# Setup as a stage of the pipeline, and the queries' root inside the exponentials of the local attention

## The chip, the cores and the metric

The kernel runs on one core of a Trainium2 chip. Its five engines are TensorE (PE, with its weight loads shown apart as PEld), VectorE (DVE), ScalarE (ACT), GpSimd (POOL) and SyncE (SP, which here only issues DMAs). Each has its own queue of instructions, works it off in order, and waits for others on semaphores. The metric is the device time of one execution in microseconds; lower is better. A kernel that differs by less than 0.3% from another isn't told from it.

## The reference

The input x has 16 sequences of 256 tokens of width 128, in fp32. Two layers, each a gated cross attention and a gated feed-forward part, with residuals:

```
x1 = x  + tanh(g_xattn[0]) * cross0(LN(x), ctx)         # 16 heads of 8, a mask on the keys
x2 = x1 + tanh(g_ffn[0])   * ffn0(LN(x1))
x3 = x2 + tanh(g_xattn[1]) * cross1(LN(x2), ctx)        # with biases
x4 = x3 + tanh(g_ffn[1])   * experts(LN(x3))            # 8 experts, the best 2, squared relu
```

ffn0 is itself a transformer of two layers. The part that matters here is its local attention, 8 heads of 64, over windows of 64 tokens, each looking at itself and the window before:

```
q, k, v = split(shift(h) @ wqkv)
q = q / |q| * q_scale ;  k = k / |k| * k_scale     # norm over each head's 64 values
q, k = rotate(q), rotate(k)                        # q also times 8
sim  = q . k, far and later positions masked
out  = softmax(sim) . v ;  h = h + out @ wo
```

## The kernel before

The 4096 tokens are 32 tiles of 128 (T = 32). Six stages work over all tiles: cross 0, local 0, mlp 0, local 1, mlp 1, cross 1, and the experts as a seventh. One loop over steps drives all engines (L1406 to L1454). Each stage has a start step (0, 34, 68, 104, 138, 173, 208), and in step s of a stage each of its operations works on tile n = s - offset; the offset is written in the code (`n = s - 5`). So each engine's queue is an order written out by hand: within a step the later stages come first, and within a stage the blocks stand in the order of the code. Stages overlap only at their ends, while one runs out and the next fills.

Ahead of the loop stands the setup (class Setup): SP and ACT issue all loads, PE makes keys and values of the context for both layers, DVE masks them. Its weights wait for one semaphore of 8 transfers, and every engine waits in `settle` for all that the setup does before it enters the loop.

The local attention on one tile (class Local), by engine, at the offsets of the kernel before:

- PE: transposes h (L839, s-1); projects queries and keys into `a_ps_qk`, three matmuls of 512 columns each (L790 to L792, s-2); transposes the rotated queries and keys (L875, s-4); projects the values (s-4); lays the mask and the scores into `a_ps_s` (L823, L806, s-5); transposes the exponentials (L847, s-6); multiplies with the values (L863, s-7); the output projection (L896, s-8).
- ACT: copies, two squares of the projections (L939, L951), and the exponentials (L932): eight instructions of 128x128, one for each head, each with a bias from `a_stat` and a sum into it.
- DVE: the rotation, four multiplies of 512 columns (L1037, L1039) and an add for the queries (L1013); the sums of squares (L988); the greatest score (L995); the inverse of the sums (L1024); copies.
- POOL: the add of the rotated keys (L1059), the roots (L1061, L1063: a power over 16 columns), the multiply of rotated queries and keys by their roots (L1067, 1024 columns), and the multiply of the exponentials by the inverse sums (L1073, 1024 columns).

The lines that set the exponentials and the multiply by the roots:

```python
act.activation(self.e[n % 2][:, P * i:P * i + P], ps_s[:, P * i:P * i + P], ACT.Exp,
               bias=stat[:, i:i + 1], accum_out=stat[:, 8 + i:9 + i]).then_inc(self.s_e, 1)
...
r = self.rot[n % 2][:, :].rearrange("p (h d) -> p h d", d=LD)
p.tensor_tensor(r, r, t[:, 48:64].unsqueeze(2).broadcast_to([P, 16, LD]), ALU.mult).then_inc(self.s_n, 1)
```

`a_ps_s` and `a_ps_t` each exist once in each layer, so the scores of a tile wait until the exponentials of the tile before have been read (`after(pe, self.s_e, 8 * k)`), and the two kinds of transposes take turns.

## Time and profile before

| | |
|---|---|
| median of 3 runs | 1317.49 us (1314.54 to 1318.94) |
| the profiled execution | 1315.28 us, its span 1313.5 us |
| mean granted TensorE clock | 0.962 of full |
| PE busy | 1142.4 us, 87% |
| PEld | 967.6 us, 74% |
| DVE | 1020.3 us, 78% |
| ACT | 913.0 us, 70% |
| POOL | 886.1 us, 67% |

The shares are means over stages with different limits: the setup is over after about 43 us, cross 0 runs to about 190 us, local 0 to about 500, mlp 0 to about 590, local 1 to about 870, and mlp 1, cross 1 and the experts fill the rest. An instruction's duration is longer than the distance to the next one on its engine, since neighbours overlap; where engines are compared, starts are what counts. Idle time of an engine that nobody waits for costs nothing.

### The profile page before, as it was taken

Reading aid. Unit: us, or ns where it says so; the run is one execution under the profiler, and the core shown is the slowest. Engines: PE = TensorE matmul, PEld = TensorE weight load, DVE = VectorE, ACT = ScalarE, POOL = GpSimd, SP = SyncE. Lnnn points to the kernel's source line nnn. Section 1 sums busy time; section 2 is a strip of 40 time slices with the busy share of each in tenths; the row PEclk is TensorE's granted clock in tenths of the full one; section 3 lists DMA queues with packets and bytes.
Section 4 is the critical chain, followed back from the end, with each engine's and each line's share of the span. In section 5 each row is a group of like instructions: output and inputs, shape, how many; then the busy total and the mean of one; then the engine's idle time right before and its main releaser. Section 6 shows DMA issues by size and latency. Waiting matters only on the chain.

```text
span 1313.5 us, 34022 instructions
## 1 busy us (share of the span) xinstructions
PE 1142.4 (87%) x11792; PEld 967.6 (74%) x11792; DVE 1020.3 (78%) x2334; ACT 913.0 (70%) x2541; POOL 886.1 (67%) x1108
## 2 busy tenths in 40 slices
PE   5388886799999988886999999979979999999997
PEld 3277764577777768885777777769867777999997
DVE  2699986788888866677888888848878887588887
ACT  1399983787777875455887777755578888666664
POOL 0688865999999983229999999943376764333442
PEclk8699997999999998997999999999989999899999
DMA  6100000000000000210011000001100000000000
GB/s 173 53 9 2 1 2 9 9 10 10 10 9 9 12 2 19 62 26 10 10 26 58 10 9 15 2 7 30 24 1 1 2 1 1 6 13 13 14 12 15
DMA packets 59417, 23.34 MB, mean 18 GB/s; under 512 B 49093, under 2 KB 57202, under 8 KB 59250
## 3 DMA queue, kind: packets, MB, share of 16 engines
q1 hardware_dynamic: 55296, 19.22, 6.0%
q10 hardware_dynamic: 3954, 1.96, 0.6%
q8 instruction: 98, 1.61, 0.5%
q14 instruction: 69, 0.57, 0.1%
HBM read 10.68 MB, written 2.10 MB: 10 GB/s over the span
## 4 chain that ended last, share of the span: by engine, by line
PE 36%; ACT 20%; DVE 19%; issue 12%; POOL 10%; ACTq 1%; DMA 1%; SPq 1%; DVEq 0%; POOLq 0%
ACT a_e L932 11%; PE m_ps_h L1275 7%; PE m_ps_y L1287 7%; DVE a_rot L1037 6%; DVE a_rot L1039 3%; PE x_ps_t L495 3%; PE a_ps_t L847 3%; ACT a_sq L939 2%; ACT x_khm L552 2%; DVE a_stat L995 2%; POOL a_stat L1063 2%; PE f_ps_y L1132 2%; POOL a_e L1073 2%; PE f_ps_g L1143 2%; PE x_ps_s L452 2%
## 5 line engine op out<-in xcount | busy, mean ns | idle before, releaser
L1063 POOL TENSOR_TENSOR a_stat<-a_stat,small 128x16 f32<-128x16 f32 x64 | 187.7, 2934 | 5.3
L932 ACT ACTIVATE a_e<-a_ps_s,a_stat 128x128 f32<-128x128 f32 x512 | 180.2, 379 | 3.2 <-DVE a_stat L995 2.4
L1073 POOL TENSOR_TENSOR a_e<-a_e,a_stat 128x1024 f32<-128x1024 f32 x64 | 121.5, 1898 | 20.0 <-DVE a_stat L1024 20.0
L1067 POOL TENSOR_TENSOR a_rot<-a_rot,a_stat 128x1024 f32<-128x1024 f32 x64 | 121.9, 1904 | 5.2 <-DVE a_rot L1013 0.3
L932 ACT ACTIVATION_READ_ACCUMULATOR a_e<-a_ps_s,a_stat 128x1 f32 x512 | 111.5, 218 | 0.0
L1037 DVE TENSOR_TENSOR a_rot<-a_ps_qk,a_rtab 128x512 f32<-128x512 f32 x128 | 87.8, 686 | 28.3 <-ACT a_sq L939 27.8
L925 ACT ACTIVATE a_eT<-a_ps_t 128x1024 f32<-128x1024 f32 x64 | 65.5, 1024 | 59.7 <-PE a_ps_t L847 57.1
L1059 POOL TENSOR_TENSOR a_rot<-a_rot 128x512 f32<-128x512 f32 x64 | 82.1, 1283 | 36.2 <-DVE a_rot L1039 34.3
L1173 ACT ACTIVATE f_gl<-f_ps_g,vec 128x128 f32<-128x128 f32 (+1 forms) x192 | 55.9, 361 | 62.7 <-PE f_ps_g L1143 62.7
L1275 PE MATMUL m_ps_h<-m_hT,w 128*128 128x128 f32 x768 | 95.1, 281 | 0.0
L1287 PE MATMUL m_ps_y<-w,m_up 128*128 128x128 f32 x768 | 91.1, 275 | 1.5 <-DVE m_yw L1322 1.5
L638 DVE TENSOR_REDUCE x_stat<-x_ps_s 128x16 f32<-128x1024 f32 x64 | 78.4, 1224 | 17.8 <-PE x_ps_s L453 17.6
L1275 PEld LDWEIGHTS m_ps_h<-m_hT,w 128*128 128x128 f32 x768 | 89.9, 195 | 0.0
L1287 PEld LDWEIGHTS m_ps_y<-w,m_up 128*128 128x128 f32 x768 | 88.3, 192 | 1.6 <-issue 1.6
L1039 DVE TENSOR_TENSOR a_rot<-a_ps_qk,a_rtab 128x512 f32<-128x512 f32 x128 | 87.1, 681 | 0.0
L1308 ACT ACTIVATE m_up<-m_ps_h 128x512 f32<-128x512 f32 x96 | 57.1, 598 | 42.3 <-PE m_ps_h L1275 42.3
L495 PE MATMUL x_ps_t<-c,x_e 128*128 128x128 f32 x512 | 73.2, 288 | 13.2 <-ACT x_e L558 13.2
L995 DVE TENSOR_REDUCE a_stat<-a_ps_s 128x8 f32<-128x1024 f32 x64 | 77.8, 1216 | 8.2 <-PE a_ps_s L806 8.2
L875 PE MATMUL a_ps_t<-c,a_rot 128*128 128x128 f32 x512 | 70.3, 282 | 15.6 <-POOL a_rot L1067 4.9
L847 PE MATMUL a_ps_t<-c,a_e 128*128 128x128 f32 x512 | 69.7, 280 | 14.6 <-POOL a_e L1073 14.5
L261 POOL TENSOR_SCALAR f_st<-f_st 128x1 f32<-128x1 f32 x64 | 14.3, 223 | 96.3 <-DVE f_st L256 95.0
L261 POOL TENSOR_SCALAR m_st<-m_st 128x1 f32<-128x1 f32 x32 | 7.3, 227 | 105.4 <-DVE m_st L256 105.4
(168 smaller groups left out, 3726.3 us busy)
## 6 DMA issues: line engine op xcount, KB each, us to landing
a_h<-y SPq DMA_DIRECT2D x64, 32.0 KB
f_h<-y SPq DMA_DIRECT2D x64, 32.0 KB
out_dram<-x SPq DMA_DIRECT2D x32, 64.0 KB, 1.5
a_h<-y SPq DMA_DIRECT2D x64, 31.8 KB
f_h<-y SPq DMA_DIRECT2D x64, 31.8 KB
wqkv<-in_L_ffn_wqkv_dram SPq DMA_DIRECT2D x2, 768.0 KB, 4.8
w<-in_L_ffn_w_dram SPq DMA_DIRECT2D x2, 768.0 KB, 5.2
c_ctx2T<-in_ctxT_dram SPq DMA_DIRECT2D x2, 512.0 KB, 3.2
```

The lines of the kernel that those rows point to most:

```text
L495: m = pe.transpose(ps_t[:, P * i:P * i + P], self.e[n % 2][:, P * i:P * i + P], g.ident)
L847: m = pe.transpose(ps_t[:, P * i:P * i + P], self.e[n % 2][:, P * i:P * i + P], g.ident)
L932: act.activation(self.e[n % 2][:, P * i:P * i + P], ps_s[:, P * i:P * i + P], ACT.Exp, bias=stat[:, i:i + 1], accum_out=stat[:, 8 + i:9 + ...
L995: v.tensor_reduce(self.stat[n % 2][:, 0:8], ps_s[:, :].rearrange("p (r k) -> p r k", k=P), AX_X, ALU.max, negate=True).then_inc(self.s_mx, 1)
L1037: v.tensor_tensor(out1, qk, cos_.unsqueeze(1).broadcast_to([P, LH, LD]), ALU.mult).then_inc(self.s_r, 1)
L1039: v.tensor_tensor(out2.rearrange("p h (o d) -> p h o d", o=2), swapped, sin_.rearrange("p (o d) -> p o d", o=2).unsqueeze(1).broadcast_to( ...
L1059: p.tensor_tensor(r, r, self.rot2[:, INNER:], ALU.add).then_inc(self.s_n, 1)
L1063: p.tensor_tensor(t[:, 48:64], t[:, 32:48], g.neg_half.broadcast_to([P, 16]), ALU.pow).then_inc(self.s_n, 1)
L1067: p.tensor_tensor(r, r, t[:, 48:64].unsqueeze(2).broadcast_to([P, 16, LD]), ALU.mult).then_inc(self.s_n, 1)
L1073: p.tensor_tensor(e3, e3, self.stat[n % 2][:, 16:24].unsqueeze(2).broadcast_to([P, 8, P]), ALU.mult)\
L1275: m = pe.matmul(self.ps_h[b][:, P * i:P * i + P], g.w1[:, P * c:P * c + P], self.hT[n % 2][:, :], start=True, stop=True)
L1287: m = pe.matmul(self.ps_y[:, D * e:D * e + D], self.up[n % 2][:, P * c:P * c + P], g.w2[:, D * c:D * c + D], start=(i == 0), stop=(i == w ...
```

## The change

It has three parts.

First, Setup becomes a stage of the loop at start 0, whose pieces stand behind those of cross 0 in steps -3 to 4. The one semaphore for weights and the `settle` ahead of the loop are gone; each consumer waits for its own load (`setup.s_id`, `setup.s_x[i]`, `setup.s_wq[l]`, ...). The local stage alone settles, on its first steps. The context is loaded once instead of twice, the masks as single rows instead of 128 copies, x in three parts; the values come in products of 128 columns, four to a bank, and layer 1's mask and key bias go into its key product as a masked context and a row of the bias.

Second, in the local attention POOL multiplies only the keys by their roots (512 columns). The queries go on unscaled; DVE multiplies the negated greatest scores by the queries' roots (8 columns), and the exponentials take that as bias and the root as scale. The mask becomes -1e24, and `a_stat` has four buffers instead of two.

Third, the blocks of the local stage stand in another sequence and at other offsets: the loads two steps ahead, all other work one step earlier, the projection of queries and keys in two blocks with their own waits. The starts of the stages become 0, 35, 67, 103, 135, 170, 205.

In the diff: the setup's products on PE, then of the local stage PE's blocks whose waits are new, ACT's exponentials, DVE's new multiply, POOL's multiply by the roots, and at the end the starts of the stages.

```diff
+    def product_k(self, pe, l, i):
+        g, src = self.g, (self.ctxT, self.ctxm)[l]
+        for j in range(2):
+            at = slice(512 * j, 512 * j + 512)
+            if l:
+                pe.matmul(self.ps_k[l][i][:, at], self.bk[:, P * i:P * i + P], self.mrow[:, at], start=True, stop=False)
+            m = pe.matmul(self.ps_k[l][i][:, at], g.wk[l][:, P * i:P * i + P], src[:, at], start=not l, stop=True)
+        m.then_inc(self.s_k, 1)
+
+    def product_v(self, pe, l, q, ps):
+
+        if l:
+            pe.matmul(ps, self.g.ones_row[:, :], self.bv[:, :].unsqueeze(1).broadcast_to([1, 4, D]), start=True, stop=False)
+        for i in range(4):
+            b = 4 * q + i
+            for lo, at, n in ((0, SC * b - SC, P),) if b else ((0, SC * (B - 1), SC), (SC, 0, SC)):
+                m = pe.matmul(ps[lo:lo + n, D * i:D * i + D], self.ctxT[:, at:at + n], self.wv[l][:, :], start=not l, stop=not l or i == 3)
+        return m
+
+    def tensor(self, pe, l, s):
+        g = self.g
+        if s == -3:
+            pe.wait_ge(self.s_key, 48)
+            for i in range(2):
+                self.product_k(pe, 0, i)
+            pe.wait_ge(self.s_val, 16)
+            for q in range(2):
+                self.product_v(pe, 0, q, self.ps_v0[q]).then_inc(self.s_vp, 1)
+        if s == 0:
+            pe.wait_ge(self.s_clear, 1)
+            pe.wait_ge(self.s_mr, 1)
+            pe.wait_ge(self.s_kl, 1)
+            for j in range(2):
+                at = slice(512 * j, 512 * j + 512)
+                m = pe.matmul(self.ps_a[:, at], g.ones_row[:, :], self.mrow[:, at], start=True, stop=True)
+            m.then_inc(self.s_bc, 1)
+            pe.wait_ge(self.s_kl, 2)
+            for q in (2, 3):
+                self.product_v(pe, 0, q, self.ps_v0[q]).then_inc(self.s_vp, 1)
+        if s in (1, 2):
+            if s == 1:
+                pe.wait_ge(self.s_val1, 32)
+            for i in range(2):
+                q = 2 * (s - 1) + i
+                if s == 1:
+                    pe.wait_ge(self.s_ve, 3 + i)
+                else:
+                    pe.wait_ge(self.s_v1, 1 + i)
+                self.product_v(pe, 1, q, self.ps_v1[q]).then_inc(self.s_vq, 1)
+        if s == 2:
+            pe.wait_ge(self.s_key1, 64)
+            pe.wait_ge(self.s_cm, 1)
+            pe.wait_ge(self.s_ve, 2)
+            self.product_k(pe, 1, 0)
+        if s == 3:
+            pe.wait_ge(self.s_kl, 3)
+            self.product_k(pe, 1, 1)
...
+        end = T * l + T
         if s == 0:
+            if not l:
+                settle(pe, self.setup.totals())
             pe.wait_ge(self.s_wh, l + 1)
             pe.wait_ge(self.s_wr, l + 1)
-        n = s - 5
+        n = s - 4
+        if 0 <= n < T:
+            k = T * l + n
+            after(pe, self.s_vc, k)
+            after(pe, self.s_oc, k - 2)
+            if n == 0:
+                self.take(pe, l, "b")
+            self.project_h(pe, ps_b[:, :], n, 1024).then_inc(self.s_v, 1)
+        n = s - 7
+        if 0 <= n < T:
+            k = T * l + n
+            pe.wait_ge(self.s_oc, k + 1)
+            after(pe, self.s_yc, k)
+            pe.wait_ge(self.s_hc, min(k + 7, end))
+            pe.wait_ge(self.s_hr, min(k + 7, end))
+            for pair in range(LP):
+                m = pe.matmul(ps_a[:, 0:D], self.oT[n % 2][:, P * pair:P * pair + P], g.lwo[:, D * pair:D * pair + D],
+                              start=(pair == 0), stop=(pair == LP - 1))
+            m.then_inc(self.s_y, 1)
...
         if 0 <= n < T:
             k = T * l + n
+            pe.wait_ge(self.s_hc, k + 1)
+            pe.wait_ge(self.s_hr, k + 1)
+            after(pe, self.s_sq, 2 * (k - 1) + 1)
+            after(pe, self.s_r, 4 * (k - 1) + 2)
+            if n == 0:
+                self.take(pe, l, "qk")
+            self.project_h(pe, ps_qk[:, 0:INNER], n, 0).then_inc(self.s_qk, 1)
+        n = s - 3
+        if 0 <= n < T:
+            k = T * l + n
+            pe.wait_ge(self.s_n, 4 * k + 4)
+            pe.wait_ge(self.s_nq, k + 1)
+            after(pe, self.s_ec, k - 2)
+            after(pe, self.s_qc, k)
+            after(pe, self.s_kc, k)
+            if n == 0:
+                self.take(pe, l, "t")
+            for i in range(2 * LP):
+                m = pe.transpose(ps_t[:, P * i:P * i + P], self.rot[n % 2][:, P * i:P * i + P], g.ident)
+            m.then_inc(self.s_t, 1)
...
+        n = s - 5
+        if 0 <= n < T:
+            k = T * l + n
+            pe.wait_ge(self.s_en, k + 1)
+            pe.wait_ge(self.s_qc, min(k + 3, end))
+            pe.wait_ge(self.s_kc, min(k + 3, end))
...
-            self.project_h(pe, ps_b[:, :], n, 1024).then_inc(self.s_v, 1)
+            self.project_h(pe, ps_qk[:, INNER:], n, INNER).then_inc(self.s_qk, 1)
...
+        n = s - 4
+        if 0 <= n < T:
+            k, stat = T * l + n, self.stat[n % UNROLL]
+            act.wait_ge(self.s_mx, 3 * k + 2)
+            after(act, self.s_et, k - 1)
+            for i in range(2 * LP):
+                e, pair = divmod(i, LP)
+                root = 48 + 2 * pair + e
+                act.activation(self.e[n % 2][:, P * i:P * i + P], ps_s[:, P * i:P * i + P], ACT.Exp, bias=stat[:, 24 + i:25 + i],
+                               scale=stat[:, root:root + 1], accum_out=stat[:, 8 + i:9 + i]).then_inc(self.s_e, 1)
...
-            act.wait_ge(self.s_mx, 2 * k + 1)
-            after(act, self.s_et, k - 1)
-            for i in range(2 * LP):
-                act.activation(self.e[n % 2][:, P * i:P * i + P], ps_s[:, P * i:P * i + P], ACT.Exp,
-                               bias=stat[:, i:i + 1], accum_out=stat[:, 8 + i:9 + i]).then_inc(self.s_e, 1)
...
+            v.wait_ge(self.s_mx, 3 * k + 1)
+            v.wait_ge(self.s_n, 4 * k + 2)
+            v.tensor_tensor(stat[:, 24:32].rearrange("p (e r) -> p e r", e=2), stat[:, 0:8].rearrange("p (e r) -> p e r", e=2),
+                            stat[:, 48:56].rearrange("p (r e) -> p e r", e=2), ALU.mult).then_inc(self.s_mx, 1)
...
-            r = self.rot[n % 2][:, :].rearrange("p (h d) -> p h d", d=LD)
-            p.tensor_tensor(r, r, t[:, 48:64].unsqueeze(2).broadcast_to([P, 16, LD]), ALU.mult).then_inc(self.s_n, 1)
...
+            r = self.rot[n % 2][:, INNER:].rearrange("p (h d) -> p h d", d=LD)
+            p.tensor_tensor(r, r, t[:, 56:64].unsqueeze(2).broadcast_to([P, LH, LD]), ALU.mult).then_inc(self.s_n, 1)
...
-        for stage, l, later in ((cross, 0, 0), (local, 0, T + 2), (mlp, 0, T + 2), (local, 1, T + 4), (mlp, 1, T + 2),
+        for stage, l, later in ((setup, 0, 0), (cross, 0, 0), (local, 0, T + 3), (mlp, 0, T), (local, 1, T + 4), (mlp, 1, T),
                                 (cross, 1, T + 3), (experts, 0, T + 3)):
             start += later
```

ACT in the middle of local 0, one step of the kernel before:

```order
L932 ACTIVATE a_e,a_stat<-a_ps_s,a_stat 128x128 x8
L939 ACTIVATE a_sq<-a_ps_qk 128x512
L945 ACTIVATE a_kTr<-a_ps_t 128x4x128
L951 ACTIVATE a_sq<-a_ps_qk 128x512
L961 ACTIVATE a_vt<-a_ps_b 128x512
L919 ACTIVATE a_hT<-a_ps_a 128x128
L925 ACTIVATE a_eT<-a_ps_t 128x1024
```

and one step of the changed kernel, where L1041 is the copy of the keys, L1048 that of h, and L1057 the exponentials:

```order
L1041 ACTIVATE a_kTr<-a_ps_t 128x4x128
L1048 ACTIVATE a_hT<-a_ps_a 128x128
L1057 ACTIVATE a_e,a_stat<-a_ps_s,a_stat 128x128 x8
L1064 ACTIVATE a_sq<-a_ps_qk 128x512
L1070 ACTIVATE a_eT<-a_ps_t 128x1024
L1028 ACTIVATE a_vx<-a_ps_b 64x512
L1029 ACTIVATE a_vt<-a_ps_b 128x512
L1035 ACTIVATE a_sq<-a_ps_qk 128x512
```

The exponentials have moved from behind the copy of the transposed exponentials to ahead of it, and the copies of keys and of h stand ahead of them.

PE at the same place, the kernel before, from the transposes of the rotated tile to the next tile's:

```order
L875 MATMUL a_ps_t<-c,a_rot 128x128 x8
L790 MATMUL a_ps_qk<-a_wqh,a_hT 128x512
L791 MATMUL a_ps_qk<-a_wqr,a_hT 128x512
L792 MATMUL a_ps_qk<-a_wqh,a_hTr 128x512
L790 MATMUL a_ps_qk<-a_wqh,a_hT 128x512
L791 MATMUL a_ps_qk<-a_wqr,a_hT 128x512
L792 MATMUL a_ps_qk<-a_wqh,a_hTr 128x512
L896 MATMUL a_ps_a<-lwo,a_oT 128x128 x4
```

and in the changed kernel, where L941 and L902 are the mask and the scores, L886 to L888 the projection, L969 the transposes of the rotated tile and L994 the product with the values:

```order
L941 MATMUL a_ps_s<-c 128x512 x2
L902 MATMUL a_ps_s<-a_kTr,a_qT 64x128 x16
L886 MATMUL a_ps_qk<-a_wqh,a_hT 128x512
L887 MATMUL a_ps_qk<-a_wqr,a_hT 128x512
L888 MATMUL a_ps_qk<-a_wqh,a_hTr 128x512
L969 MATMUL a_ps_t<-c,a_rot 128x128 x8
L994 MATMUL a_ps_b<-a_eT,a_vt 64x64 x16
L1005 MATMUL a_ps_t<-c,a_e 128x128 x8
L886 MATMUL a_ps_qk<-a_wqh,a_hT 128x512
L887 MATMUL a_ps_qk<-a_wqr,a_hT 128x512
L888 MATMUL a_ps_qk<-a_wqh,a_hTr 128x512
```

Between scores and transposes of the rotated tile now stands the queries' half of the projection alone; the keys' half has moved behind the transposes of the exponentials. No matmul of the local stage is added or lost.

## Rows read from the trace of the kernel before

**Rows 1.** The page's first part: busy time of each engine

```profile
PE 1142.4 (87%) x11792; PEld 967.6 (74%) x11792; DVE 1020.3 (78%) x2334; ACT 913.0 (70%) x2541; POOL 886.1 (67%) x1108
```

**Rows 2.** Timeline of the first 60 us: start us, us, engine, line, instruction

```profile
13.18 3.60 PE L346 MATMUL c_ps_k<-c_ctx2T,wk 128*128 128x512 f32 x8
...
24.83 6.36 PE L346 MATMUL c_ps_k<-c_ctx2T,wk 128*128 128x512 f32 x8 [5.89 <-DVE kT L361]
...
53.75 0.77 PE L452 MATMUL x_ps_s<-x_khl,x_qhh 128*128 128x512 f32 x1 [0.76 <-DVE x_qlm L652]
```

**Rows 3.** DMA issues: KB each, median us to landing

```profile
wk<-in_L_xattn_WkT_dram ACTq DMA_DIRECT2D x4, 64.0 KB, 6.0
```

**Rows 4.** Timeline of POOL: first and last root multiply of each layer

```profile
213.36 1.91 POOL L1067 TENSOR_TENSOR a_rot<-a_rot,a_stat 128x1024 f32<-128x1024 f32 x1
...
481.64 1.90 POOL L1067 TENSOR_TENSOR a_rot<-a_rot,a_stat 128x1024 f32<-128x1024 f32 x1
...
597.35 1.90 POOL L1067 TENSOR_TENSOR a_rot<-a_rot,a_stat 128x1024 f32<-128x1024 f32 x1
...
858.49 1.90 POOL L1067 TENSOR_TENSOR a_rot<-a_rot,a_stat 128x1024 f32<-128x1024 f32 x1
```

**Rows 5.** Timeline of POOL over one step of local 1

```profile
612.56 1.90 POOL L1073 TENSOR_TENSOR a_e<-a_e,a_stat 128x1024 f32<-128x1024 f32 x1
614.41 1.27 POOL L1059 TENSOR_TENSOR a_rot<-a_rot 128x512 f32<-128x512 f32 x1
...
615.99 2.93 POOL L1063 TENSOR_TENSOR a_stat<-a_stat,small 128x16 f32<-128x16 f32 x1
618.99 1.91 POOL L1067 TENSOR_TENSOR a_rot<-a_rot,a_stat 128x1024 f32<-128x1024 f32 x1
```

**Rows 6.** Timeline of PE in local 0, with idle time ahead in brackets

```profile
302.82 0.47 PE L790 MATMUL a_ps_b<-a_wqh,a_hT 128*128 128x512 f32 x1
...
303.61 0.60 PE L823 MATMUL a_ps_s<-c 128*128 128x512 bf16 x2
...
305.82 0.30 PE L839 MATMUL a_ps_a<-c,a_h 128*128 128x128 f32 x1 [0.58 <-DVE y L1045]
...
308.22 1.06 PE L875 MATMUL a_ps_t<-c,a_rot 128*128 128x128 f32 x8
...
312.11 0.60 PE L823 MATMUL a_ps_s<-c 128*128 128x512 bf16 x2
```

**Rows 7.** Timeline of DVE in the same step, its two waits

```profile
311.04 0.20 DVE L1024 RECIPROCAL a_stat<-a_stat 128x8 f32<-128x8 f32 x1 [1.01 <-ACT a_e L932]
311.63 0.69 DVE L1037 TENSOR_TENSOR a_rot<-a_ps_qk,a_rtab 128x512 f32<-128x512 f32 x1 [0.38 <-ACT a_sq L939]
```

**Rows 8.** Timeline of ACT: a tile's first exponential, and what follows the eighth

```profile
299.47 0.37 ACT L932 ACTIVATE a_e<-a_ps_s,a_stat 128x128 f32<-128x128 f32 x1
...
302.23 0.64 ACT L939 ACTIVATE a_sq<-a_ps_qk 128x512 f32<-128x512 f32 x1
302.70 0.65 ACT L945 ACTIVATE a_kTr<-a_ps_t 128x512 f32<-128x512 f32 x1
```

**Rows 9.** Groups of ACT by shape: count, busy us, mean ns, idle before

```profile
L932 ACT ACTIVATE a_e<-a_ps_s,a_stat 128x128 f32<-128x128 f32 x512 | 180.2, 379 | 3.2 <-DVE a_stat L995 2.4
L932 ACT ACTIVATION_READ_ACCUMULATOR a_e<-a_ps_s,a_stat 128x1 f32 x512 | 111.5, 218 | 0.0
...
L1165 ACT ACTIVATE f_hT<-f_ps_x,vec 128x128 f32<-128x128 f32 x64 | 29.3, 458 | 14.0 <-PE f_ps_x L1122 13.8 <-issue 0.2
...
L566 ACT ACTIVATE x_qhh<-x_ps_q,small 128x128 fp32r<-128x128 f32 x64 | 19.8, 360 | 8.3 <-PE x_ps_q L464 8.2
...
L919 ACT ACTIVATE a_hT<-a_ps_a 128x128 fp32r<-128x128 f32 x64 | 17.7, 277 | 73.4 <-PE a_ps_a L839 73.3
```

**Rows 10.** Timeline of ACT while mlp 0 runs alone

```profile
530.45 0.88 ACT L1173 ACTIVATE f_gl<-f_ps_g,vec 128x128 f32<-128x128 f32 x3 [0.88 <-PE f_ps_g L1143]
...
532.55 0.87 ACT L1173 ACTIVATE f_gl<-f_ps_g,vec 128x128 f32<-128x128 f32 x3 [0.88 <-PE f_ps_g L1143]
```

548 lines of the change are left out of this document (273 added, 275 removed).

## Prediction

> **What bounds the kernel now.** I read the page's first part first [rows 1]: PE 87%, DVE 78%, ACT 70%, POOL 67%. These are means over seven stages, so they don't say what bounds the local attention, where most of the change lies. The timeline does. POOL's multiply by the roots starts at 213.36 us for the first tile of local 0 and at 481.64 for the last; in local 1 at 597.35 and 858.49 [rows 4]. These are 31 steps each: 268.3 / 31 = 8.65 us a step and 261.1 / 31 = 8.42. In such a step POOL hardly rests [rows 5]: from the multiply of the exponentials at 612.56 it is 1.85 us to the add, 1.58 to the power (a small maximum lies between), 3.00 to the multiply by the roots, and that multiply takes 1.86 to its follower, 8.29 in all. So POOL bounds the local attention, and with 62 steps of some 8.5 us it is 40% of the time.
>
> The other three are close behind. PE comes from one tile's masks at 303.61 to the next one's at 312.11 in 8.50 us, of which one wait on DVE is 0.58 [rows 6]; as every block also begins with a gap of some tenths, I take 7.8 us as the least PE needs. DVE waits 1.01 and 0.38 us in a step [rows 7], so it needs 8.50 - 1.39 = 7.1. ACT does the eight exponentials in 302.23 - 299.47 = 2.76 us [rows 8], and its idle time in a step is about 1.5 us, so it needs 6.9 to 7.0 (an estimate from its timeline; the row of the copy of h alone has 73.4 us of idle over 64 steps, 1.15 each [rows 9]).
>
> The start is a chain of its own [rows 2]: key products from 13.18 us on, the second layer's only at 24.83, at half the clock (6.36 us for what took 3.60), and then masks; the first scores of cross 0 come at 53.75 us.
>
> **The local step after the change.** POOL: the multiply by the roots falls from 1024 to 512 columns. Half of 1.90 is 0.95, the least; the add of the same 512 columns with two full inputs takes 1.27 [rows 5], the most. The row nearest in kind is the multiply with a repeated operand, so I take 0.97 and POOL's sum is 8.29 - 0.90 = 7.4 us (7.35 to 7.7).
>
> DVE: one more multiply of 8 columns. The nearest row is the reciprocal of 8 columns, 0.20 us [rows 7]; it must also wait for the maximum just before it to be written. I take 0.25 (0.1 to 0.4): 7.35 us.
>
> ACT: the exponentials get a second operand from SBUF. The trace has no exponential with both, but it has 128x128 instructions from PSUM with none, one and two such operands: 277, 360 and 458 ns [rows 9]. So the scale costs 98 ns each, 8 x 0.098 = 0.78 us a step, 3.54 instead of 2.76. The bounds: 0, if the read of the accumulator (218 ns, half hidden now) covers it; 2.0 us, if the pair of 379 + 218 ns no longer overlaps. I take the row's 0.78, and ACT's sum is 7.7 us. So most of what POOL is spared in time (0.90 a step) is paid again on ACT; it is hidden only as far as ACT idled.
>
> The Trainium skill, "ScalarE: Activation LUTs", in the part on what an ACT_TABLE_LOAD costs, has a rule that speaks against this edit: each per-partition pointer operand of an ACTIVATE adds about 93 ns. By it the sum for ACT would be 8 x 0.093 = 0.74 us a step. It agrees with the three rows; that the price also holds in time to the next instruction, and for an exponential with a sum, no run here shows.
>
> PE: the same matmuls in the local stage, one more block to start: 7.8 to 7.9. Its wait for DVE's addition to y (0.58) goes, since the output projection now stands well ahead of the transpose of h that needs its bank.
>
> So POOL 7.4, DVE 7.35, ACT 7.7, PE 7.8: level, and what decides is the chain between them. Follow a tile from its masks at 0. Masks and scores end at 305.24 - 303.61 = 1.63 (the wait before 305.82 began then). The queries' half of the projection adds 0.79 (the three value matmuls from 302.82 to 303.61 are the same kind), the eight transposes 1.06 (0.8 to the next block), all [rows 6]: they end at about 3.4. Then ACT copies the keys (0.47 to the next, as at 302.23 to 302.70 [rows 8]) and h (0.2), and starts the exponentials at 4.1; the greatest scores (1.2 us behind the scores) and the new multiply are ready by 3.2, so they are off this chain. 3.54 later, at 7.65, the eighth is done, and with 0.1 for the semaphore the next masks may start: 7.75. PE comes to the same point at 7.8. DVE's own round, entered by its wait for the same transposes, gives 7.75 too. In the kernel before, the exponentials also stood behind the copy of the transposed ones, which waits for POOL's multiply; that dependence is gone, which is why the step can follow POOL down at all.
>
> With all four level each small delay of one is felt by all; I add 0.15 and forecast 7.95 us a step (bounds 7.5, where only the sums of POOL and DVE count, and 8.4, where the exponentials cost 0.5 more). Local 0 runs its first five steps beside the end of cross 0, whose own root operations on POOL stay, so it keeps some 3 us: 268.3 - 31 x 7.95 - 3 = 19; local 1: 261.1 - 31 x 7.95 = 15. Sum 34 us.
>
> **The setup.** The first scores need: the key weights (issued by ACT first now; a landing takes 6.0 us [rows 3], so PE starts near 7.5 instead of behind eight transfers), then PE's work. A 512-column matmul in fp32 costs 3.60 / 4 = 0.90 us at the full clock and 6.36 / 4 = 1.59 at the lower [rows 2]. Ahead of the first scores stand 4 key products for layer 0, 4 for layer 1 with their bias rows, 2 to spread the mask row, 4 rows of value bias: 14 x 0.90 = 12.6, and 34 value products of 128 columns at a quarter, 7.6. That is 20 us, against 14.4 before; the price of the new form is 6 us of PE. The waits between (mask rows landed, the low parts of the keys, DVE's masked values before their banks are free) add 4 to 5. So the first scores come at 32 at the full clock and at 44 if half of it runs at the lower. I take 36, and lose 1.5 again as the last four key products (3.6 us) now lie among the first steps of cross 0, whose PE is not full. Gain 53.75 - 36 - 1.5 = 16 us; bounds 8 and 22. The final `settle` of the local stage, 30 steps later, waits for nothing.
>
> What SP queues now ahead of the attention weights (some 30 issues instead of 9) is needed at step 4 of cross 0 or later, and the attention weights at step 32: hidden, 0; should x's second part be late, cross 0 waits 1 to 3 us once.
>
> **The ends of the stages.** The loop has three steps less. Each makes one step in which an mlp ran alone one that is shared with the local attention. Alone such a step takes 532.55 - 530.45 = 2.10 us [rows 10]: 6.3 us, less about 2 for the work that now lies in a fuller step. I take 4 (bounds 10 and -4; the conversion of the attention weights, now two and three steps earlier, falls into cross 0's full steps instead of an emptier one).
>
> **Sum.** From the profiled execution: 1315.28 - 34 - 16 - 4 = 1261 us, and its median's scale is 0.2% higher; I stay with 1261.
>
> **The rivals.**
>
> 1. The step falls to the sums of POOL and DVE, 7.5 us: the semaphore gaps that I counted on PE overlap, and the scale is half hidden behind the accumulator's read. For it: four banks of statistics and earlier loads give slack. Against it: PE's 7.8. Local saving 529.4 - 62 x 7.5 - 3 = 61: 1315 - 61 - 16 - 4 = 1234.
> 2. ACT keeps the old pace. The exponentials cost 1.2 us more instead of 0.78, since the new operand can't be read while the accumulator is; the chain masks, projection, transposes, copies, exponentials becomes 8.3. Local saving 529.4 - 62 x 8.35 - 3 = 9: 1286.
> 3. Slower: the same chain at its worst. If ACTIVATE and accumulator read no longer overlap, eight pairs take 8 x (379 + 98 + 218) = 5.6 us, the step 4.1 + 5.6 + 0.1 = 9.8, and the local stages lose 62 x (9.8 - 8.54) = 78: about 1373. It turns to slower than before where the step exceeds 8.54 + 20 / 62 = 8.86, that is where a pair costs over 0.58 us instead of 0.345 now. Against it: the rows with one and two operands differ by 98 ns and not by more.
> 4. The setup doesn't shorten: PE idles long enough between its pieces to run at the lower clock throughout, as from 24.83 us now, and DVE's chain of waits does the rest. First scores at 48, gain 4: 1273.
>
> **Chances.** The forecast 0.60 (own range 1246 to 1276), rival 1 0.14, rival 2 0.14, rival 4 0.06, rival 3 0.04, and 0.02 for no change by two errors that cancel. What a measurement can tell from no change is 0.3%, 4 us. Faster 0.94, same 0.02, slower 0.04. The range leaves out rival 3 and the outer part of 1 and 2: 1230 to 1290.
>
> **What would show it.** Right: starts of the keys' root multiply 7.8 to 8.1 us apart in both local stages, that multiply near 0.97 us, the exponentials near 475 ns and eight of them in 3.5 us, PE's wait for y gone and its idle time in local 0 under 5%, POOL busy for less than 7.6 us of a step there; first scores at 32 to 44 us. Wrong: a step at 8.4 with ACT busy throughout (rival 2), a step at 7.5 (rival 1), or stretches of cross 0 slower than before by more than 3 us, which I counted at nothing.

## The result, and the profile after

| | kernel before | changed kernel |
|---|---|---|
| median of the runs shown | 1316.39 us (1314.54 to 1318.94, 4 runs) | 1271.01 us (1258.75 to 1272.81, 4 runs) |
| profiled execution | 1315.28 us, span 1313.5 | 1272.81 us, span 1270.9 |
| mean granted clock of TensorE | 0.962 | 0.960 |

The ratio is 0.9641, with a 95% interval of 0.9608 to 0.9673: 45 us faster. I had forecast 1261 us, so the time lies 10 us above it, inside both ranges. One of the four runs was at 1258.75 us, with a mean clock of 0.974 where the others had 0.960 to 0.967; that difference inside one kernel gave the first hint of the cause below.

The page's first part after, to set beside [rows 1]. PE has 24.5 us more of busy time, for 56 more instructions; that is more than their work.

```profile
PE 1166.9 (92%) x11848; PEld 983.7 (77%) x11848; DVE 1026.1 (81%) x2368; ACT 955.8 (75%) x2545; POOL 859.6 (68%) x1110
```

The timeline of POOL, first and last multiplication of the keys by their root in each layer, as in [rows 4]:

```profile
214.56 1.38 POOL L1200 TENSOR_TENSOR a_rot<-a_rot,a_stat 128x512 f32<-128x512 f32 x1
...
464.57 1.04 POOL L1200 TENSOR_TENSOR a_rot<-a_rot,a_stat 128x512 f32<-128x512 f32 x1
...
572.94 1.04 POOL L1200 TENSOR_TENSOR a_rot<-a_rot,a_stat 128x512 f32<-128x512 f32 x1
...
818.39 1.04 POOL L1200 TENSOR_TENSOR a_rot<-a_rot,a_stat 128x512 f32<-128x512 f32 x1
```

These four starts and the span cut both kernels into the same five pieces, and the differences add up to the whole:

| piece | before | after | difference | forecast |
|---|---|---|---|---|
| start to the first such multiplication (setup, cross 0) | 213.4 | 214.6 | +1.2 | -16 |
| 31 steps of local 0 | 268.3 | 250.0 | -18.3 | -19 |
| from local 0 to local 1 (mlp 0) | 115.7 | 108.4 | -7.3 | -4, with the last piece |
| 31 steps of local 1 | 261.1 | 245.4 | -15.7 | -15 |
| from there to the end of the span | 455.0 | 452.5 | -2.5 | |

So the local attention gave what was forecast, the ends of the stages gave more, and the setup gave nothing. Over 31 steps the local attention goes from 8.65 to 8.06 us a step in local 0, and from 8.42 to 7.92 in local 1; in the middle of both stages it goes from 8.57 to 7.86. The first steps of the stages make the difference.

**The step of the local attention.** POOL over one step, as in [rows 5]:

```profile
299.49 1.44 POOL L1200 TENSOR_TENSOR a_rot<-a_rot,a_stat 128x512 f32<-128x512 f32 x1
300.90 1.89 POOL L1182 TENSOR_TENSOR a_e<-a_e,a_stat 128x1024 f32<-128x1024 f32 x1
302.76 0.24 POOL L1189 TENSOR_SCALAR a_stat<-a_stat 128x16 f32<-128x16 f32 x1
303.09 2.92 POOL L1192 TENSOR_TENSOR a_stat<-a_stat,small 128x16 f32<-128x16 f32 x1
305.98 1.29 POOL L1194 TENSOR_TENSOR a_rot<-a_rot 128x512 f32<-128x512 f32 x1
307.36 1.44 POOL L1200 TENSOR_TENSOR a_rot<-a_rot,a_stat 128x512 f32<-128x512 f32 x1
```

307.36 - 299.49 = 7.87 us, and POOL doesn't wait. PE in the same step, as in [rows 6]:

```profile
299.86 0.59 PE L941 MATMUL a_ps_s<-c 128*128 128x512 bf16 x2
...
302.22 1.03 PE L969 MATMUL a_ps_t<-c,a_rot 128*128 128x128 f32 x8
303.09 0.27 PE L980 MATMUL a_ps_a<-c,a_h 128*128 128x128 f32 x1
...
307.72 0.59 PE L941 MATMUL a_ps_s<-c 128*128 128x512 bf16 x2
```

From masks to masks 7.86 us, and no row has a wait in brackets: the 0.58 us for DVE's addition to y [rows 6] is gone. Two engines without a pause in one step don't tell which of them sets it; that takes an experiment. DVE's one wait of note in that step, to set beside [rows 7], and the addition of the rotated queries, which now begins 0.16 us before POOL's multiplication:

```profile
303.29 0.69 DVE L1133 COPY a_qT<-a_ps_t 128x512 f32<-128x512 f32 x1 [0.31 <-PE a_ps_t L969]
...
307.20 0.69 DVE L1164 TENSOR_TENSOR a_rot<-a_rot 128x512 f32<-128x512 f32 x1
```

ACT's first exponential and what follows the eighth, as in [rows 8]; and its groups by shape, as in [rows 9]:

```profile
303.94 0.46 ACT L1057 ACTIVATE a_e<-a_ps_s,a_stat 128x128 f32<-128x128 f32 x1
...
307.42 0.64 ACT L1064 ACTIVATE a_sq<-a_ps_qk 128x512 f32<-128x512 f32 x1
```

```profile
L1057 ACT ACTIVATE a_e<-a_ps_s,a_stat 128x128 f32<-128x128 f32 x512 | 226.7, 477 | 4.5 <-DVE a_stat L1126 4.4
L1057 ACT ACTIVATION_READ_ACCUMULATOR a_e<-a_ps_s,a_stat 128x1 f32 x512 | 115.8, 226 | 0.0
```

Eight exponentials take 3.48 us (2.76 before; forecast 3.54). One takes 477 ns, 98 more than before. The other two groups of rows hardly differ: the key weights land after 4.5 us (6.0 in [rows 3]), and a step of the mlp alone takes 2.11 us (2.10 in [rows 10]).

**The start.** PE in the first 60 us, to set beside [rows 2]. `1*128 1x512` is a product of one row: a bias, or the mask's row, spread over a tile. The trace records each fp32 product of the setup as two instructions, so `x2` is one product of 512 columns.

```profile
25.95 2.07 PE L349 MATMUL c_ps_b<-c_bv,ones_row 1*128 1x512 f32 x2 [0.75 <-ACT vall L410]
27.95 2.08 PE L353 MATMUL c_ps_b<-c_wv,c_ctxT 128*128 128x128 f32 x8
...
39.98 2.08 PE L343 MATMUL c_ps_c<-c_ctxm,wk 128*128 128x512 f32 x2
41.06 1.42 PE L531 MATMUL x_ps_s<-x_khl,x_qhh 128*128 128x512 f32 x1
...
47.70 2.07 PE L342 MATMUL c_ps_c<-c_mrow,c_bk 1*128 1x512 f32 x2 [3.52 <-DVE kT L421]
```

The first scores stand at 41.06 us, 12.7 earlier than before. But the gain is gone one tile later. DVE's maxima of the first three tiles of cross 0, before and after:

```profile
55.83 1.23 DVE L638 TENSOR_REDUCE x_stat<-x_ps_s 128x16 f32<-128x1024 f32 x1 [1.77 <-PE x_ps_s L453]
60.00 1.22 DVE L638 TENSOR_REDUCE x_stat<-x_ps_s 128x16 f32<-128x1024 f32 x1 [0.94 <-PE x_ps_s L453]
64.03 1.22 DVE L638 TENSOR_REDUCE x_stat<-x_ps_s 128x16 f32<-128x1024 f32 x1 [0.94 <-PE x_ps_s L453]
```

```profile
43.66 1.23 DVE L729 TENSOR_REDUCE x_stat<-x_ps_s 128x16 f32<-128x1024 f32 x1 [17.38 <-PE x_ps_s L532]
57.35 1.22 DVE L729 TENSOR_REDUCE x_stat<-x_ps_s 128x16 f32<-128x1024 f32 x1 [8.04 <-PE x_ps_s L532]
62.97 1.22 DVE L729 TENSOR_REDUCE x_stat<-x_ps_s 128x16 f32<-128x1024 f32 x1 [0.93 <-PE x_ps_s L532]
```

12.2 us ahead at the first tile, 1.1 at the third. Between them stand the last key products, from 47.70 us on. They first wait 3.52 us, then run at half the clock. The wait is a chain through one place in PSUM: both halves of layer 1's keys go through `c_ps_c`, so PE may write the second half only when ACT has copied the first and DVE has subtracted that copy, and ACT comes to this behind its copies for the first tile and of the values:

```profile
45.34 1.05 ACT L397 ACTIVATE kT<-c_ps_c 128x1024 fp32r<-128x1024 f32 x1
46.41 1.23 DVE L421 TENSOR_TENSOR kT<-c_ps_c,kT 64x1024 fp32r<-64x1024 f32 x1 [1.21 <-ACT kT L397]
```

The windows of 26 to 42 and 42 to 58 us after (length, then busy us of PE, PEld, DVE, ACT, POOL, then TensorE's granted clock, DMA share, GB/s):

```profile
26.00:42.00 16.00, 16.00 (x29) 7.00 (x30) 0.24 (x2) 1.98 (x4) 5.41 (x8) 0.50 0.24 60
42.00:58.00 16.00, 12.48 (x30) 6.03 (x29) 5.03 (x7) 4.19 (x8) 2.27 (x7) 0.64 0.00 0
```

PE works 16.00 of 16.00 us, and is granted 0.50, the level of 1.2 GHz. The Trainium skill, "TensorE: Matmul & The Clock Gate", section "Why this matters for your kernels", advises to keep TensorE busy without a pause for the full rate. This trace differs, and the measurement decides: the stretch has no pause. What sets it apart from stretches at 1.00 may be what PE works on; the experiments below test that.

### The profile page after: what moved, and what is told of

Read it like the earlier page. It is cut to its first block, busy times and chain, and to the rows that moved or that the text cites. A ratio compares the mean times of both kernels' runs of the same rounds, so it can differ in the third digit from the quotient of the medians.

```text
span 1270.9 us, 34469 instructions
## 1 busy us (share of the span) xinstructions
PE 1166.9 (92%) x11848; PEld 983.7 (77%) x11848; DVE 1026.1 (81%) x2368; ACT 955.8 (75%) x2545; POOL 859.6 (68%) x1110
## 4 chain that ended last, share of the span: by engine, by line
PE 71%; ACT 8%; DVE 7%; issue 7%; POOL 4%; SPq 1%; DMA 1%; ACTq 0%; DVEq 0%; POOLq 0%
PE m_ps_h L1401 7%; PE m_ps_y L1413 7%; PE a_ps_s L902 5%; PE a_ps_b L994 5%; PE a_ps_t L1005 5%; PE a_ps_t L969 4%; PE a_ps_a L929 4%; PE a_ps_qk L886 3%; PE x_ps_t L575 3%; PE a_ps_s L941 2%; ACT x_khm L636 2%; PE a_ps_qk L888 2%; PE a_ps_qk L887 2%; PE x_ps_s L531 2%; PE f_ps_g L1269 2%
## 5 line engine op out<-in xcount | busy, mean ns | idle before, releaser
L1057 ACT ACTIVATE a_e<-a_ps_s,a_stat 128x128 f32<-128x128 f32 x512 | 226.7, 477 | 4.5 <-DVE a_stat L1126 4.4
L1057 ACT ACTIVATION_READ_ACCUMULATOR a_e<-a_ps_s,a_stat 128x1 f32 x512 | 115.8, 226 | 0.0
L1200 POOL TENSOR_TENSOR a_rot<-a_rot,a_stat 128x512 f32<-128x512 f32 x64 | 90.1, 1407 | 5.0
L1194 POOL TENSOR_TENSOR a_rot<-a_rot 128x512 f32<-128x512 f32 x64 | 82.9, 1296 | 7.2 <-DVE a_rot L1080 7.1
L1115 DVE TENSOR_REDUCE a_stat<-a_sq 128x16 f32<-128x1024 f32 x64 | 77.8, 1215 | 1.2 <-ACT a_sq L1064 1.1
L575 PEld LDWEIGHTS x_ps_t<-c,x_e 128*128 128x128 f32 x512 | 57.1, 145 | 27.5 <-ACT x_e L642 19.8
L902 PEld LDWEIGHTS a_ps_s<-a_kTr,a_qT 64*64 64x64 f32 x2048 | 55.8, 134 | 27.9 <-issue 27.9
```

The source lines that it names most:

```text
L575: m = pe.transpose(ps_t[:, P * i:P * i + P], self.e[n % 2][:, P * i:P * i + P], g.ident)
L902: return pe.matmul(dst, self.qT[u][rows, P * pair + WIN * x:P * pair + WIN * x + WIN], ky, start=False, stop=(pair == LP - 1))
L1194: p.tensor_tensor(r, r, self.rot2[:, INNER:], ALU.add).then_inc(self.s_n, 1)
L1200: p.tensor_tensor(r, r, t[:, 56:64].unsqueeze(2).broadcast_to([P, LH, LD]), ALU.mult).then_inc(self.s_n, 1)
```

## The experiments

Each kernel is the changed kernel with one edit, unless it says otherwise. In the local attention I read the step as the mean distance of POOL's multiplications of the exponentials over some 16 steps in the middle of each layer, since the total also carries what the clock does at the start.

### The two parts apart

`local_alone` is the kernel before with the class of the local attention, the mask's constant and the starts of the stages from the changed one:

```
...
-((cross, 0, 0), (local, 0, T + 2), (mlp, 0, T + 2), (local, 1, T + 4), (mlp, 1, T + 2),
+((cross, 0, 0), (local, 0, T + 3), (mlp, 0, T), (local, 1, T + 4), (mlp, 1, T),
...
```

> The kernel before with the changed local attention alone (its order on each engine, the root as scale, the mask's constant, the starts of the stages), and the setup of before. If the gains of the two parts add up as the stretches of the two traces say (18.3 and 15.6 us in the two local stages, 7.5 between local and MLP of layer 0, 2.5 in the rest), this takes 1271 to 1275 us, since the setup gave 1.5 us there and took 2.7 us back at the start of the local stage. Had the setup's part given what I forecast (16 us), and the local part less, it would be 1283 to 1287 us.

Measured: 1269.23 us (1267.82 to 1270.01), ratio 0.9639 [0.9622, 0.9655]. That is the whole gain of the change, from the local part and the starts alone. Its five pieces are 213.7, 250.0, 107.9, 245.8 and 450.2 us. So the new setup as it stands is worth nothing, and its cost isn't hidden somewhere later either. No run tells the two halves of the local part apart, the root as scale of the exponentials and the new order of the blocks: what each is worth of the 34 us isn't shown.

### What holds the setup back

`rows128` gives the one-row products 128 rows, 127 of them zeros:

```
-self.ones_row = sb("ones_row", P, F32, 1)
+self.ones_row = sb("ones_row", P, F32)
...
-self.bv, self.bk = self.sb("bv", D, F32, 1), self.sb("bk", 2 * D, F32, 1)
+self.bv, self.bk = self.sb("bv", D, F32), self.sb("bk", 2 * D, F32)
...
+for t in (self.bv, self.bk, self.mrow):
+    v.memset(t[:, :], 0.0).then_inc(self.s_zr, 1)
...
-pe.matmul(ps, self.g.ones_row[:, :], self.bv[:, :].unsqueeze(1).broadcast_to([1, 4, D]), ...)
+pe.matmul(ps, self.g.ones_row[:, :], self.bv[:, :].unsqueeze(1).broadcast_to([P, 4, D]), ...)
...
```

> The changed kernel with one edit in the setup: the products that spread a row (the mask's row, and layer 1's biases of keys and values) take 128 rows, the row itself and 127 rows of zeros, in place of one row. Columns and output are the same; three VectorE memsets are added. Theory A (the granted clock): in the changed kernel PE works without a pause from about 26 to 57 us but is granted 0.50 in most of it, and the stretches at 0.50 are those with one-row products; with 128 rows the clock is 1.0 from about 30 us on, the second tile's statistics come some 8 to 14 us earlier, and the kernel takes 1257 to 1263 us. Rival B (the work): the setup's stage is as long as its products and the waits between engines make it, rows or not; then nothing moves, 1269 to 1273 us, and the clock stays at 0.50 in the same stretches.

Measured: 1258.42 us (1257.97 to 1258.87), ratio 0.9557 [0.9542, 0.9573], so 11 to 13 us less than the changed kernel (by the ratios, and by the medians), with more work in it. Its windows:

```profile
26.00:42.00 16.00, 12.48 (x39) 6.61 (x38) 4.38 (x6) 5.27 (x10) 7.42 (x16) 0.89 0.36 100
42.00:58.00 16.00, 12.62 (x110) 10.22 (x111) 12.66 (x24) 12.10 (x22) 9.37 (x17) 0.89 0.01 3
```

and the products at its start:

```profile
25.88 1.02 PE L351 MATMUL c_ps_b<-c_bv,ones_row 128*128 128x512 f32 x2
26.74 1.05 PE L355 MATMUL c_ps_b<-c_wv,c_ctxT 128*128 128x128 f32 x8
...
36.23 2.06 PE L344 MATMUL c_ps_c<-c_mrow,c_bk 128*128 128x512 f32 x2 [3.52 <-DVE kT L423]
38.09 1.82 PE L345 MATMUL c_ps_c<-c_ctxm,wk 128*128 128x512 f32 x2
39.75 1.02 PE L344 MATMUL c_ps_c<-c_mrow,c_bk 128*128 128x512 f32 x2
```

The same product takes 1.02 us where it took 2.07. From 22 us on the clock falls only behind PE's two long waits, the 3.52 us ahead of 36.23 and one of 3.01 us ahead of 47.00, and each time it comes back among the matmuls that follow. The first scores are at 30.67 us and the first multiplication by the root at 200.8: 10.4 and 13.7 us ahead of the changed kernel. Against the kernel before, the first piece is 12.6 us shorter, where I had forecast 16.

The clock isn't all that the start lacks. DVE's maxima of the first and the third tile of cross 0 in `rows128`:

```profile
32.20 1.22 DVE L734 TENSOR_REDUCE x_stat<-x_ps_s 128x16 f32<-128x1024 f32 x1 [7.84 <-PE x_ps_s L537]
...
49.08 1.23 DVE L734 TENSOR_REDUCE x_stat<-x_ps_s 128x16 f32<-128x1024 f32 x1 [1.81 <-PE x_ps_s L537]
```

These are 16.9 us apart, against 8.2 in the kernel before and 19.3 in the changed one. So of the 11.1 us of lead that the changed kernel loses between them, 8.7 are lost with 128 rows too: the wait for `c_ps_c`, which is 3.52 us here as well, the key products themselves, and the next wait. The clock costs 2.4 us there, and most of its price, 10.4 us, lies ahead of the first scores.

`rows1ctl` is the control: the tiles, memsets and waits of `rows128`, with the products back on one row.

```
...
-self.bk[:, P * i:P * i + P], self.mrow[:, at]
+self.bk[0:1, P * i:P * i + P], self.mrow[0:1, at]
...
```

> Control for rows128: the same tiles of 128 rows, the same three memsets, the same wait ahead of the loads of the biases, but the products take the first row alone. Theory A (a one-row product doesn't hold the granted clock up): the clock is back at 0.50 from 26 to 57 us and the time is that of the changed kernel, 1268 to 1273 us. Rival F (rows128 gained by the memsets' or loads' moved times, or by where the products fell): 1257 to 1261 us as rows128.

Measured: 1270.30 us (1269.26 to 1271.83), ratio 0.9665 [0.9636, 0.9695], and its windows are back near where they were, at 0.60 and 0.54:

```profile
26.00:42.00 16.00, 15.73 (x37) 7.54 (x37) 1.43 (x3) 2.33 (x6) 5.95 (x10) 0.60 0.38 108
42.00:58.00 16.00, 12.06 (x25) 5.89 (x25) 5.70 (x8) 5.72 (x11) 3.71 (x8) 0.54 0.00 0
```

Its first scores are at 37.97 us and its first and third maxima 21.0 us apart (40.70 and 61.71), so against this control the clock costs 7.3 us ahead of the first scores and 4.1 between those maxima. So it is the rows and nothing that came with them. Theory A holds; rivals B and F fall.

`nobias` leaves the eight bias products out:

```
-    pe.matmul(self.ps_k[l][i][:, at], self.bk[:, P * i:P * i + P], self.mrow[:, at], start=True, stop=False)
...
-    pe.matmul(ps, self.g.ones_row[:, :], self.bv[:, :].unsqueeze(1)..., start=True, stop=False)
```

> The changed kernel without layer 1's bias rows in the products of keys and values (8 one-row products of 512 columns left out of the computation). Theory A (the granted clock, as for rows128): the one-row product that spreads the mask stays, the others go, so the clock comes back by about 35 us and 8 products of 1.04 us at full clock go as well; the kernel takes 1253 to 1261 us, less than with 128 rows. Rival B (the work): only the 8 products go, at 2.07 us each from the trace 16.6 us, and the clock stays at 0.50 in the rest; 1254 to 1262 us. The clock of the stretch from 30 to 55 us tells them apart, not the time.

Measured: 1250.24 us (1248.57 to 1254.02), ratio 0.9499 [0.9477, 0.9521]. The two windows show 0.76 and 0.81 instead of 0.50 and 0.64, so the clock is up for part of the stretch, as theory A has it. It falls behind PE's waits of 3.52 us (until 31.98) and 3.02 us (until 42.08), with no one-row product near: waits and rows both bring it down. Its first piece is 195.7 us, 5.1 us less than in `rows128`, for eight products that take 6.9 us of PE there (0.86 each from start to start): with the clock up, most of what they take of PE is what they cost. The totals differ by 8.2 us, but 2.6 of that lies in the last piece, where the two kernels are the same. Between the first and the third maximum it still takes 16.2 us, so the loss there isn't the bias products either.

`rows32` is `rows128` with the products on the first 32 rows.

> As rows128, but the products take the first 32 rows, one with data and 31 of zeros. It asks whether the clock follows the number of rows that a product takes. If any product of several rows will do: 1257 to 1261 us and the clock 1.0 from 26 us on, as with 128. If the rows count in proportion: the clock stays at 0.50 through most of 26 to 57 us, 1265 to 1273 us.

Measured: 1261.36 us, but from 1259.13 to 1268.40 us. The profiled run is the slowest of the four and has 0.57 and 0.68 in the two windows; the other three had mean clocks of 0.968 to 0.976 (the profiled one 0.966). So 32 rows sometimes do and sometimes don't. Judged by their times, for only one execution of each kernel has a trace, one row did in one run of four of the changed kernel (1258.75) and in none of four of the control; 128 rows did in all 13 runs of `rows128`, `early` and `vbias` (1253.36 to 1258.87). How the clock depends on the number of rows in between stays open.

### What sets the step

`poolless` multiplies 2 of 8 heads of the keys by their root, `peless` leaves out one of the three products of each projection, `bothless` does both, `noscale` leaves the scale out of the exponentials:

```
# poolless
-r = self.rot[n % 2][:, INNER:].rearrange("p (h d) -> p h d", d=LD)
-p.tensor_tensor(r, r, t[:, 56:64].unsqueeze(2).broadcast_to([P, LH, LD]), ALU.mult)
+r = self.rot[n % 2][:, INNER:INNER + INNER // 4].rearrange("p (h d) -> p h d", d=LD)
+p.tensor_tensor(r, r, t[:, 56:58].unsqueeze(2).broadcast_to([P, 2, LD]), ALU.mult)
# peless
-pe.matmul(dst, h[:, :], self.wqr[:, lo:lo + 512], start=False, stop=False)
...
# noscale
-bias=stat[:, 24 + i:25 + i], scale=stat[:, root:root + 1],
+bias=stat[:, i:i + 1],
```

> The changed kernel with POOL's multiplication of the keys by their root on 2 of the 8 heads (128 of 512 columns; 6 heads are left unmultiplied), about 0.9 us a step less on POOL, so that its five instructions need about 6.9 us. Theory P (POOL, without a pause in the step of 7.86 us, sets it): the step falls to what PE needs, by 0.1 to 0.4 us, 1246 to 1265 us. Theory E (PE sets it): POOL now waits and the step stays at 7.86, 1268 to 1273 us.

> The changed kernel without the middle product (high part of the activations by low part of the weights) in the projections of the local attention: three products of 512 columns a step left out, about 0.7 us of PE. Theory P (POOL sets the step): 7.83 to 7.86 us stay, 1266 to 1273 us, and PE now waits. Theory E (PE sets it): the step falls by 0.1 to 0.5 us until POOL's 7.83 us or VectorE's 7.55 us hold it; 1250 to 1268 us.

> Both edits at once (POOL's multiplication on 2 of 8 heads; no middle product). If POOL and PE are both at their sums, each alone gives nothing or little and the two together give 0.3 us a step or more, until VectorE (7.55 us of its queue in the step of 7.86) or the exponentials hold it: step 7.5 to 7.6 us, 1248 to 1256 us. If a chain through all engines sets the step, the gain is the sum of the two single gains.

> The changed kernel with the exponentials' scale left out (the root of the queries isn't applied; the bias is the unscaled maximum), so that an exponential has one pointer less: 94 ns less each by the two traces, 0.75 us a step on ACT. If ACT lies off the path in the step, as its 75% busy share says, nothing moves: 7.86 us, 1268 to 1273 us. If the chain from the maxima through the exponentials to POOL sets the step, it falls by 0.2 to 0.7 us, 1228 to 1258 us.

| kernel | time, us | ratio, 95% | step, us | busy from 300 to 400 us: PE, DVE, ACT, POOL |
|---|---|---|---|---|
| changed | 1271.01 | 0.9641 [0.9608, 0.9673] | 7.86 | 100.0, 93.8, 93.0, 98.0 |
| `poolless` | 1263.56 | 0.9592 [0.9561, 0.9623] | 7.86 | 100.0, 94.1, 93.4, 85.0 |
| `peless` | 1266.56 | 0.9615 [0.9585, 0.9645] | 7.78 | 95.7, 99.1, 94.4, 97.9 |
| `bothless` | 1260.04 | 0.9556 [0.9514, 0.9597] | 7.63 | 97.2, 96.8, 95.5, 88.0 |
| `noscale` | 1264.42 | 0.9622 [0.9596, 0.9648] | 7.83 | 100.0, 94.5, 84.0, 98.0 |

In `poolless` POOL now waits in every step, and the step doesn't move:

```profile
301.56 0.40 POOL L1200 TENSOR_TENSOR a_rot<-a_rot,a_stat 128x128 f32<-128x128 f32 x1
302.95 1.90 POOL L1182 TENSOR_TENSOR a_e<-a_e,a_stat 128x1024 f32<-128x1024 f32 x1 [0.98 <-DVE a_stat L1105]
```

So PE sets the 7.86 us (theory E). With 0.7 us taken from PE the step falls by 0.08 only: PE is then at 95.7, and POOL does its round in the same 7.78 us without a wait in brackets, with DVE at 99.1. With both relieved it falls by 0.23, not by 0.08 + 0: POOL is a bound of its own right behind PE. I had expected 0.3 or more there. In `bothless` POOL waits for DVE in each step and PE for ACT, and PE and DVE are both near 97; that a chain through these engines sets 7.63 is argued from this, not shown. ACT with 0.74 us less gives 0.03. The totals of this group scatter by 6 to 13 us within a kernel (`poolless` 1257.77 to 1270.31), too much to read the step from; the medians of `poolless`, `bothless` and `noscale` lie outside the ranges that I had set for what their steps then showed, and by its total alone `poolless` would have spoken for theory P. The profiled run of `poolless`, its slowest, has its first piece at 219.3 us instead of 214.6; 2.9 us of that stand at its first scores already (43.97 us), and its clock is at 0.50 from 22 to 46 us. The steps in the middle of the two local stages agree to 0.01 us in each kernel.

`addmove` puts DVE's addition of the rotated queries one step later, under POOL's power:

```
-        n = s - 1
+        n = s - 2
         if 0 <= n < T:
             k, r = T * l + n, self.rot[n % 2][:, 0:INNER]
             v.wait_ge(self.s_r, 4 * k + 2)
             v.tensor_tensor(r, r, self.rot2[:, 0:INNER], ALU.add).then_inc(self.s_nq, 1)
```

(the block stands behind the multiplication of the maxima instead of at the end of DVE's step)

> The changed kernel with one edit in the local attention: VectorE's addition of the rotated queries (0.69 us, two SBUF inputs) is put one step later, behind the multiplication of the maxima, so that it lies beside POOL's power (16 columns, 2.9 us) as in the kernel before, and no longer beside POOL's multiplication by the root. Theory C (the two share a path to SBUF): POOL's multiplication falls from 1.44 us to 0.97 to 1.05 us. If POOL's sum sets the step of 7.86 us, the step falls by 0.4 us over 62 steps, 1246 to 1252 us; if PE sets it, POOL's time falls and the step and the kernel stay, 1268 to 1273 us. Rival D (the slower multiplication is its operand, 8 heads in place of 16 with the same spread): it stays at 1.4 us.

Measured: 1281.37 us (1274.03 to 1285.20), ratio 0.9715 [0.9691, 0.9738]: slower than the changed kernel. POOL over one step of it:

```profile
301.10 2.93 POOL L1192 TENSOR_TENSOR a_stat<-a_stat,small 128x16 f32<-128x16 f32 x1
304.48 1.29 POOL L1194 TENSOR_TENSOR a_rot<-a_rot 128x512 f32<-128x512 f32 x1 [0.45 <-DVE a_rot L1080]
305.85 1.05 POOL L1200 TENSOR_TENSOR a_rot<-a_rot,a_stat 128x512 f32<-128x512 f32 x1
306.92 1.90 POOL L1182 TENSOR_TENSOR a_e<-a_e,a_stat 128x1024 f32<-128x1024 f32 x1
```

The multiplication falls to 1.05 us as theory C says; D falls. But both of my times were wrong: the step goes up to 8.03 us. The addition now stands on DVE ahead of the rotation of the keys, so that POOL's addition of the keys (L1194) waits 0.45 us for it in each step. In the two local stages this costs 9.5 us (254.4 and 250.5 against 250.0 and 245.4); the first piece is 5.5 us longer too (220.0), of which 2.8 stand at the first scores already (43.90 us), where the edit hasn't come into play. So the order on DVE was worth more than POOL's 0.4 us.

### Towards a faster version

`early` is `rows128` with layer 0's preparation of the local attention seven steps earlier:

```
-        if s == -3:
+        if s == (-3 if l else -10):
...
```

> rows128 with layer 0's preparation of the local attention (the copy of its weights on ACT, the rotation tables and the low part of the weights on VectorE, the memsets on POOL) seven steps earlier in the cross attention, out of the last steps in which PE is busy for 1.4 of 5 us (165 to 170 us of rows128). If they are what delays the last steps, the first multiplication by the root comes 2 to 3 us earlier and the kernel takes 1255 to 1257 us. Rival: each costs the same wherever it stands in the cross attention, whose engines are all near 90% busy, or its wait for the weights blocks them: 1258 to 1262 us.

Measured: 1255.03 us (1254.64 to 1255.56), ratio 0.9547 [0.9519, 0.9574]. The stretch of 165 to 170 us, `rows128` first, then `early`:

```profile
165.00:170.00 5.00, 1.38 (x8) 1.03 (x7) 4.40 (x10) 3.84 (x6) 3.31 (x6) 0.94 0.18 37
```

```profile
165.00:170.00 5.00, 4.37 (x55) 3.35 (x47) 4.55 (x11) 4.79 (x10) 4.48 (x12) 1.00 0.02 5
```

The hole in PE is closed, but the first multiplication by the root moves from 200.8 to 199.7 only, 1.1 us. The last piece is 2.5 us shorter (450.2 against 452.7), and there the two kernels are the same. So most of the 3.4 us between the medians isn't this edit's, and the two intervals overlap.

`vbias` is `early` with the values' bias added by DVE as it takes them out of PSUM:

```
-act.activation(g.vall[1][:, 512 * q:512 * q + 512], self.ps_v1[q], ACT.Copy)
+v.tensor_tensor(g.vall[1][:, 512 * q:512 * q + 512]..., self.ps_v1[q]..., self.bv[:, :].unsqueeze(1).broadcast_to([P, 4, D]), ALU.add)
```

> early, and layer 1's bias of the values out of PE: its four products of 512 columns (1.04 us each at full clock by nobias against rows128, 2.07 at half) go, and VectorE adds the bias, loaded to all rows, as it takes the values out of PSUM (four additions of 0.68 us in place of ACT's four copies). nobias took 8 us less than rows128 with 8 products fewer, so four should give 2 to 4 us where PE sets the stage: 1250 to 1254 us. Rival: VectorE is what the first tiles of the cross attention wait for from 30 us on, and the additions there give it back: 1254 to 1257 us.

Measured: 1256.60 us (1253.36 to 1256.76), ratio 0.9540 [0.9524, 0.9557]. Its first maximum comes at 29.0 us against 32.2 and its first multiplication by the root at 198.3 against 199.7, so less than half of what it gains at the start is left at the end of cross 0, and the total can't tell it from `early`. All three of `rows128`, `early` and `vbias` are faster than both kernels, by 4.3 to 4.8% against the one before by the ends of their intervals; which of the three is best isn't settled.

## Why the prediction was right, and where it was wrong

- **The local step: right, its fit to a tenth of a microsecond luck.** Forecast 7.95 us as the mean of 31 steps, with 3 us more in local 0; measured 7.86 in the middle of both layers, and 8.06 and 7.92 as the means. Saved 18.3 + 15.7 = 34.0 us for a forecast of 34, and `local_alone` has 18.3 + 15.3. Two misses cancel in it: 62 steps at 7.86 are 5.6 us shorter than at 7.95, and the first steps of the stages cost 6.4 + 1.8 us more than that instead of 3. Rivals 1, 2 and 3 are out: no step at 7.5, and a pair of exponential and accumulator read takes 0.44 us, not 0.58.
- **PE at 7.8 as the largest sum: right**, and shown by `poolless` and `peless` (7.86, with POOL at 7.78 behind it). PE's wait for y is gone.
- **ACT's price: right.** 98 ns for an operand, as read from three other shapes [rows 9]; eight exponentials 3.48 for 3.54.
- **POOL's multiplication: mis-sized.** I took 0.97 us, in a bound of 0.95 to 1.27, and it is 1.44 (median of 64: 1.442) while DVE adds from SBUF beside it, 1.04 without. POOL is busy for 7.7 us of a step (97.97% of 7.86), over the 7.6 that I had named as a sign, and its round without a wait takes 7.78 (`peless`) instead of 7.4. It cost nothing, since PE needs 7.86, but with it POOL is the bound as soon as PE is relieved.
- **The setup: the step that failed.** I wrote "I take 36, and lose 1.5 again as the last four key products (3.6 us) now lie among the first steps of cross 0, whose PE is not full", a gain of 16; measured -1.2. Two terms of it were off.
  - The first scores came at 41.06 us instead of 36, inside my 32 to 44. With the clock held up (`rows128`) they come at 30.67. The difference, 10.4 us (7.3 from the control `rows1ctl`), is what the one-row products cost ahead of the first scores, by leaving TensorE at 0.50. I had also priced a product at the lower level at 1.59 us, from a group in which the clock rose; one takes 2.00 us there (25.95 to 27.95).
  - The term of 1.5 is the one that failed in its mechanism. By the third tile 11.1 us of the lead were gone. The four products took 8 us instead of 3.6, and ahead of them PE waited 3.52 us for ACT and DVE to leave `c_ps_c`, a wait that I had put at nothing. With the clock mostly back the loss is still 8.7 us, so the larger part is the wait and the work behind it and the smaller part the clock. No run takes that wait away, as a second place in PSUM would, so what it costs by itself stays open.

  This is also my sign of being wrong, "stretches of cross 0 slower than before by more than 3 us": from the first maximum to the first multiplication by the root it takes 170.9 us instead of 157.5. In size the setup is rival 4, which had 0.06 (first scores at 48, gain 4). Its reason was half right: DVE's chain of waits is there, but up to the first scores PE idled for 0.75 us in all between its pieces, and what left it at 0.50 was what it worked on.
- **The ends of the stages: low.** Forecast 4, measured 7.3 + 2.5 = 9.8, at the edge of my bounds (10 and -4). `local_alone` has 7.8 + 4.8 in the same two pieces, which is outside them; the last piece varies by 2.8 us between profiles of kernels that are the same there (450.0 in `rows1ctl`, 452.8 in `vbias`).
- **The sum.** 1261 was 12 us below the profiled execution: 17 too much for the setup, 6 too little for the ends. That the total fell within 1% is in part luck, since these two have opposite signs. The median is 2 us under that execution.
